# Attention scores of the head mixture: k's low part padded from 64 to 128 rows

## The reference

```
q = einsum('bte,bted->btd', rw, einsum('btc,ecd->bted', x, q_proj))
k = einsum('bte,bted->btd', rw, einsum('btc,ecd->bted', x, k_proj))
v = einsum('bte,bted->btd', rw, einsum('btc,ecd->bted', x, v_proj))
scores = einsum('bqd,bkd->bqk', q, k) / sqrt(64)
scores = where(causal, scores, -inf)
attn = einsum('bqk,bkd->bqd', softmax(scores), v)
```

## Time and profile before

| what | value |
|---|---|
| median of three runs | 4489.09 us |
| the profiled execution's own time | 4494.44 us |
| its span | 4492.6 us |
| mean granted TensorE clock | 0.925 of full speed |
| TensorE matmuls busy | 80% of the span |
| VectorE busy | 72% |
| GpSimd busy | 40% |
| ScalarE busy | 31% |

### The profile page before, as it was taken

The page is one execution under the profiler, slowest core; times in us unless marked ns, Lnnn a source line. Parts: engine busy times, 40 slices in busy tenths (PEclk is TensorE's granted clock), DMA queues, the critical chain, the costliest instruction groups (busy, mean ns, idle before and its releaser), DMA issues. The chain is left out here.

```text
span 4492.6 us, 39616 instructions
## 1 busy us (share of the span) xinstructions
PE 3576.0 (80%) x13112; PEld 2012.1 (45%) x13168; DVE 3243.8 (72%) x4803; ACT 1407.8 (31%) x2360; POOL 1796.4 (40%) x874
## 2 busy tenths in 40 slices
PE   5799879987988798777778677777777786777769
PEld 2577557765766486632223322224322233222234
DVE  4566456545754476469997679995699976799955
ACT  3222322232223222253332343331533323433310
POOL 1101210121003000309995049991099950499910
PEclk9899989998989899899999889998999998899989
DMA  3000100010001000206663136661066631366530
GB/s 126 1 19 1 57 1 10 10 57 1 1 20 58 1 1 19 90 11 217 209 206 131 34 123 211 210 202 61 10 218 209 207 131 35 122 209 209 204 107 7
DMA packets 156471, 421.74 MB, mean 94 GB/s; under 512 B 21713, under 2 KB 58961, under 8 KB 154465
## 3 DMA queue, kind: packets, MB, share of 16 engines
q1 hardware_dynamic: 156258, 419.03, 27.4%
HBM read 392.20 MB, written 26.78 MB: 93 GB/s over the span
## 5 line engine op out<-in xcount | busy, mean ns | idle before, releaser
L1376 POOL TENSOR_TENSOR hc<-h,c_sb 128x1024 f32<-128x1024 f32 x344 | 806.0, 2352 | 622.5 <-DMA c_sb<-bc_rows 550.7
L1304 PE MATMUL PS<-hc,ident 128*128 128x512 f32 x1376 | 712.4, 644 | 89.7 <-POOL hc L1376 75.0
L1345 ACT ACTIVATE da<-dt,a_neg 128x1024 f32<-128x1024 f32 x384 | 437.7, 1141 | 501.5 <-DVE h L1401 501.4
L1287 PE MATMUL PS<-bc,pick 128*128 128x512 bf16 x712 | 237.5, 414 | 300.6 <-DVE h L1401 265.8
L1384 DVE TENSOR_TENSOR PS<-dtu,PS 128x1024 f32<-128x1024 f32 x384 | 461.4, 1202 | 5.4 <-PE PS L1287 5.4
L1304 PEld LDWEIGHTS PS<-hc,ident 128*128 128x128 f32 x1376 | 257.7, 200 | 425.2 <-issue 207.8
L1401 DVE TENSOR_TENSOR_SCAN h<-da,state,PS 128x1024 f32<-128x1024 f32 x192 | 443.3, 2328 | 0.0
L1401 DVE TENSOR_TENSOR_SCAN h<-da,PS 128x1024 f32<-128x1024 f32 x192 | 431.3, 2268 | 0.0
L100 POOL TENSOR_TENSOR ln_rstd<-ln_var,eps_pow 128x4 f32<-128x4 f32 x65 | 71.4, 1105 | 849.8 <-DVE ln_var L93 849.8
L689 DVE SCALAR_TENSOR_TENSOR acc<-PS,rw,acc 128x192 f32<-128x192 f32 x768 | 285.0, 413 | 174.5 <-ACT acc L721 91.1
L1376 POOL TENSOR_TENSOR tok<-h,c_sb 128x1024 f32<-128x1024 f32 x168 | 395.1, 2352 | 33.7 <-DVE h L1401 24.5
(11 more groups left out here) (251 smaller groups left out, 6552.1 us busy)
## 6 DMA issues: line engine op xcount, KB each, us to landing
c_sb<-bc_rows SPq DMA_DIRECT2D x512, 512.0 KB, 4.2
bu<-bc_rows SPq DMA_DIRECT2D x64, 512.0 KB, 5.4
tok<-bc_rows SPq DMA_DIRECT2D x64, 512.0 KB, 5.5
xT<-in_xT SPq DMA_DIRECT2D x5, 2048.0 KB, 7.5
tok<-in_x SPq DMA_DIRECT2D x4, 2048.0 KB, 9.6
x_after_layer<-tok SPq DMA_DIRECT2D x16, 512.0 KB, 3.0
xT_after_layer<-x2T_out SPq DMA_DIRECT2D x16, 512.0 KB, 2.8
x2T<-xT_after_layer SPq DMA_DIRECT2D x16, 512.0 KB, 3.7
```

Of the source, the lines that this page charges most:

```text
L1287: op = pe.matmul(bank(at + j), pick[:, row, :], bc3[:, half * HALF + j * CHUNK:half * HALF + (j + 1) * CHUNK], start=True, stop=True)
L1304: op = pe.matmul(bank(Y + j), ident[:, :], hc_at[v % 3][:, j * CHUNK:(j + 1) * CHUNK], start=(n == 0), stop=(n == N - 1))
L1345: act.activation(decay_at(v), dt[:, m, at], ACT.Exp, scale=a_neg[:, n:n + 1]).then_inc(dr, 1)
L1376: pool.tensor_tensor(hc_at[v % 3], h[:, v % 3, :], c_sb[:, v % 3, :], ALU.mult).then_inc(hr, 1)
```

## The change

`k_lo` gets 128 rows. Rows 64 to 127 are zeroed with the rest of the tile by a memset on GpSimd, once per batch, after the second `xlo`; a new semaphore `k_lo_zeroed` makes VectorE wait for it ahead of the first tile's low parts. VectorE writes k's low part to rows 0 to 63 as before. The second pass of a score now takes all 128 rows of `q_parts` against `k_lo`, the same weights as the first pass; the low part of q meets zeros there.

```diff
-    k_lo = tile(heads, "k_lo", [EHD, SEQ], F32R)
+
+    k_lo = tile(heads, "k_lo", [P, SEQ], F32R)
...
+        kz = sem("k_lo_zeroed")
...
                     pool.tensor_tensor(xlo[:, i % 2, :, :], xT[:, :, i * P:(i + 1) * P],
                                        xhi[:, i % 2, :, :].bitcast(F32), ALU.subtract).then_inc(lo, 1)
+                    if i == 1:
+                        pool.memset(k_lo[:, :].bitcast(F32), 0.0).then_inc(kz, 1)
...
                     dve.wait_ge(qc, i + 1)
+                    if i == 0:
+                        dve.wait_ge(kz, 1)
...
-                    dve.tensor_tensor(k_lo[:, at], bank(6 + i % 2)[0:EHD, P:2 * P], k_hi2[0:EHD, at].bitcast(F32),
+                    dve.tensor_tensor(k_lo[0:EHD, at], bank(6 + i % 2)[0:EHD, P:2 * P], k_hi2[0:EHD, at].bitcast(F32),
                                       ALU.subtract).then_inc(ql, 1)
...
-                        last = pe.matmul(bank(c)[:, 0:keys], q_parts[0:EHD, tile_q], k_lo[:, at], start=False,
+                        last = pe.matmul(bank(c)[:, 0:keys], q_parts[:, tile_q], k_lo[:, at], start=False,
                                          stop=not diagonal)
```

## The result

The changed kernel takes 4441.59 us (median of four runs, 4435.09 to 4444.03) against 4488.90 us for the kernel before (four runs). The ratio is 0.9893, with an interval of 0.9876 to 0.9910: 47 us faster. The forecast was 36 us, with 4441 us as the low end of the range, so the result lies at that edge. The mechanism held; the forecast gain was too small by almost a quarter.

A forecast was written before the change was run, and what follows sets the result against it. TensorE's chain was taken to bound the four attention stages, 8% of the span. Tiles 6 to 15 (6.3 us) plus tiles 0 to 5 (2.8 us) gave 9.1 us a stage, 36 us in all: 4453 us, range 4441 to 4472, forecast 80%.

The forecast's parts named there:

- part (a): All 80 score boundaries per batch become 128-row, 0.20 us less at 2.4 GHz; at most 17 us a stage.
- part (b): Tiles 6 to 15: VectorE's maxima, spaced 0.67 us, become the slower and leave a gain of 6.3 us a stage.
- the sum: Tiles 6 to 15 6.3 us plus tiles 0 to 5 2.8 us: 9.1 us a stage, 36 us for four.
- part (c): Tiles 0 to 5, mostly at 1.2 GHz: 1.8 + 0.4 + 1.6 - 1.0 for the clock = 2.8 us a stage.
- part (d): GpSimd memset of k's low part, 0.95 to 1.9 us per batch, hidden in idle time; cost nothing.
- No gain: Rival: the exposed load in the scores has another cause, so nothing moves, 4489 us; 8%.
- Half: Rival: only one of two boundary kinds in the scores goes, 6.5 us a stage, 4463 us; 8%.
- The clock: Rival: TensorE's clock rises only 60 us into each stage, 6.4 us a stage slower, 4515 us; 4%.
- an earlier rise: Within the forecast: clock rising 7 us sooner in each attention stage brings 2.5 us a stage, 4443 us.

The follow-up runs named there:

- e1: Kernel before with both score passes over 64 rows, the product of q's low part with k's high part left out: 4461.24 us, ratio 0.9939.
- e2: Kernel before with each tile's 128-row passes all first and its 64-row passes behind them: 4480.25 us, ratio 0.9986.
- e5: VectorE's maxima over each chunk's last 128 keys only, in both kernels: 4412.35 us on the changed one, 4477.23 us on the one before.
- e7: Changed kernel plus matmuls nobody reads, around the mixture's last transposes and in tiles 0 to 3: 4433.40 us, ratio 0.9881.
- e8: Kernel before plus the same matmuls nobody reads: 4471.06 us, ratio 0.9965.
- e3: Changed kernel with clearing, semaphore and wait kept, but the second pass over 64 rows again: 4480.13 us, ratio 0.9981.
- e4: Changed kernel run once more, nothing altered: 4441.15 us, ratio 0.9891.
- e11: Changed kernel with rows 64 to 127 of k's doubled high part also zeroed, q-low by k-high product left out: one run, 4434.22 us.

## Why the prediction came out as it did

*The bound and the boundary, part (a).* Right, but for the first pass of a tile. The spacings of 0.23 us at 2.4 GHz (0.20 us less) and of 0.43 us at 1.2 GHz stand in the profile after, and e1 and e2 show that the boundary carries the cost: not the 64-row form (e1), and not the number of 64-row passes (e2). Of the Trainium skill's two rules, the one of "TensorEngine Tiling (Array Packing)", Key Properties, that a change of the tiling mode drains TensorE, fits: each change of rows costs 0.20 us. The one of "TensorE: Matmul & The Clock Gate", Part 3, that a load overlaps matmuls only when its row group differs, did not hold: loads for the same rows overlap at 0.23 us a pass in the scores too.

*VectorE as the next limit, part (b).* The mechanism was right: the gap between the pairs of e5 shows it as 4.7 us a stage. **This is the step that failed, by the size of one term.** I took 0.67 us as VectorE's spacing, from two maxima in a row at 382.74 in the earlier trace rows. But the second of these was tile 12's last chunk and waited for TensorE's mask. The merged row could not show that: maxima that wait for nothing are 0.69 us long and start 0.60 us apart, so they overlap by 0.09 us, and a wait of 0.07 us leaves no idle time between two. VectorE's own spacing is 0.60 us. With it a further full chunk brings 0.26 us and not 0.19, and a last chunk 0.07, 0.19, 0.31 and 0.43 us; worked as before, four-chunk tiles give 3.9, three-chunk tiles 2.8 and the two others 1.1 us, 7.9 us for tiles 6 to 15 where I had 6.3. The trace shows 8.1 in the first batch. These three rows, tile 6's start before, and tile 6's and tile 15's now, give most of it:

```profile
345.96 0.48 PE L770 MATMUL PS<-k_hi,q_parts 128*128 128x512 f32 x1
```

```profile
342.79 0.48 PE L776 MATMUL PS<-k_hi,q_parts 128*128 128x512 f32 x1
...
393.90 0.48 PE L776 MATMUL PS<-k_hi,q_parts 128*128 128x512 f32 x1
```

From tile 6 to tile 15 it was 404.06 - 345.96 = 58.10 us and is 393.90 - 342.79 = 51.11 us, 7.0 less; tile 15 to the end of the stage gives 1.1 more. Over the four stages tiles 6 to 15 gave 32.7 us, where the sum had 25.2: 7.5 of the 10.6 us that were missing. The spacing by itself accounts for 4 x (7.9 - 6.3) = 6.4 us of them.

*The tiles at the lower clock, part (c).* 2.8 us a stage forecast. The first batch has 345.96 - 325.59 = 20.37 us before and 342.79 - 325.42 = 17.37 us now: 3.0 us, and it is 3.0 to 4.7 us in the four stages, 14.2 in all for the 11.2 of the sum, which is the other 3 us. Two errors partly cancel. The one-chunk tiles give 1.4 us (tiles 0 to 3) and not 2.2: their first pass takes 0.59 us to the next where I had 0.43, so 0.13 us is saved there for the 0.30 that I counted. And I charged 1.0 us for a clock that would keep its time; it came 4 to 10 us sooner instead. e7 and e8 put the clock's part at 7.3 us in all, 1.8 a stage; with the clock alike, tile 6 starts 15.26 us into e7's first stage and 16.99 into e8's, so the passes give 1.7 us of the mean of 3.5. The clock's price of 0.36 us for a us held in e3 at 16 to 21 us into the stage, but not at 11 to 13 us, where e4's stages are alike to 0.1 us. Where the clock rises at 11.1 us, TensorE is done early and waits 0.89 us for ScalarE's exponential ahead of tile 5:

```profile
338.94 0.50 PE L776 MATMUL PS<-k_hi,q_parts 128*128 128x512 f32 x1 [0.89 <-ACT prob L859]
```

Where it rises at 13.0 us, in the third stage, TensorE starts tile 5 without a wait, 0.03 us later.

*Clearing, part (d).* Right: 1.80 us, inside the 0.95 to 1.9, and hidden (e3).

*The rivals.* No gain: out, by the spacing. Half: out, both kinds of boundary fell to 0.23 us. (Its sum has 1.2 us for half of (c)'s 2.8, which is 1.4: 4462 us and not 4463.) The clock: it moved, and the other way; why it rises sooner in the changed kernel stays open. I had weighed longer waits as a reason for a delay, and an earlier rise only as the low end. TensorE's wait in tile 15 grew to 0.92 us, not 1.2: with VectorE's 0.60 us the last maximum comes 1.15 us sooner and not 0.94, and the eight boundaries save 1.50 us (3.41 us from the first pass to the mask before, 1.91 now) and not 1.6, since the first pass keeps 0.31 us.

## What to carry to other kernels

Matmuls that contract over 128 and over 64 rows should not alternate where TensorE is the limit: every change from one to the other left a weight load in the open here, 0.20 us at 2.4 GHz and up to 0.30 us at 1.2 GHz for loads of 128 columns. Other numbers of rows were not measured. Fill the smaller one up with zeros if its pass takes no longer for it, or group the passes, if what waits for the first of them can bear it. When an engine's spacing is to be the next limit, take it from a run of instructions in which none waited; a merged row of two with a wait too short to show gave 0.67 us for 0.60 here, and that alone was 6.4 of the 10.6 us of error.

## What the runs showed that I had not expected

The rise of TensorE's clock moved with the form of the score passes. It came at 20.0 to 20.3 us into the stage with 64-row scores and two boundaries a tile (e1), at 16.4 to 21.3 us with 128 and 64 rows alternating (before and e3), and at 10.8 to 13.2 us with 128 rows and no boundary, whether the added rows hold data or zeros (the changed kernel, e4 and e11). Between the late and the early rises the rows addressed and the boundaries changed together, so which of the two counts is not shown. A kernel that has 64-row passes without any boundary, or boundaries at equal rows addressed, would have to tell. Some 60 small matmuls per batch, 36 at the mixture's end and 25 in the waits of tiles 0 to 3, kept the clock at 2.4 GHz through all four stages (e7, 1.00 against 0.93), for 8 us, although nothing reads what they compute. Whether fewer would do was not tried.
